# One product of the first mixture of experts as a single float32 matmul in place of three split ones

## The chip, the cores and the metric

The kernel runs on 1 core of one Trainium2 chip. The metric is device time in microseconds (us). A profile is one execution, recorded instruction by instruction. TensorE, the matrix engine, is called PE in it (PEld is its weight load); DVE is the vector engine, ACT the scalar engine, POOL the GpSimd engine, and SP the engine that only issues transfers here.

## The reference

Two decoder layers work on x of 8 x 128 tokens with 128 features. Each layer is attention, cross attention and a feed-forward part, each behind a layer norm. The change is in the feed-forward part of the first layer, a mixture of 16 experts with 8 chosen for each token and one shared expert:

```python
gates = jnp.einsum('bsd,ed->bse', x, gate_w)
scores = jax.nn.sigmoid(gates.astype(jnp.float32))
_, inds = jax.lax.top_k(scores + expert_bias, K)
selected = jnp.take_along_axis(scores, inds, axis=-1)
selected = selected / selected.sum(axis=-1, keepdims=True) * ROUTE_SCALE
combine = jnp.einsum('bske,bsk->bse', jax.nn.one_hot(inds, E), selected)
hg = jnp.einsum('bsd,eid->bsei', x, w_gate)
hu = jnp.einsum('bsd,eid->bsei', x, w_up)
h = jax.nn.silu(hg) * hu
ye = jnp.einsum('bsei,edi->bsed', h, w_down)
y = jnp.einsum('bsed,bse->bsd', ye, combine)
y = y + einsum(silu(x @ shared_gate_w.T) * (x @ shared_up_w.T), shared_down_w)
```

All sizes are 128 (features and hidden units), so each weight matrix is 128 x 128.

## The kernel before

The parts of the network run one after the other. Inside one, each engine runs its own instruction list, and semaphores order them. The first mixture is `mixture0`. All 16 experts are computed for all 1024 tokens, with the hidden layer multiplied by the routing weight, which is zero for the tokens that did not choose the expert. The shared expert is the 17th, number 16.

The tokens are cut into two halves of 512 columns. A **unit** u is one expert and one half: u = 2 x expert + half, so there are 34 units, 0 to 33. For each unit PE makes these products:

* `first_products`: the gate and the up product. Each operand is split in two parts, high and low, of the type F32R, and a product is three matmuls, high x high, high x low and low x high (`product`, lines 870 to 872).
* `weights`: one bf16 matmul that spreads the routing weights of the expert over all partitions (L884). The shared expert has none.
* `last_product`: the down product of `h`, three matmuls again, which add into one PSUM bank per half over all 17 experts.

PE's order is written out by hand: first products of u, weights of u, last product of u - 2. The last product thus runs two units behind, that is one expert behind. The lists of ACT and DVE follow the same order. For a unit ACT makes `g` = silu(gate) (L934), DVE `t` = up x g (L1007) and `h` = t x routing weight (L1012). Then ACT makes `h_hi` (L940, a copy to F32R) and DVE `h_lo` = h - h_hi (L1049). The buffers `g`, `t`, `h`, `h_hi`, `h_lo` exist twice, one for each half.

The weights of an expert (gate, up, down, 192 KB) are loaded by one transfer of SP into `w[j]`, j = expert modulo 2 (L862; the shared expert's is L865). POOL splits them into `w_hi[j]` and `w_lo[j]`: gate and up together (128 x 256) for the first products, which are told by `w_split`, and down (128 x 128), told by `down_split`. Both have a high step (L976) and a low step (L978). SP loads expert e when POOL has split the down matrix of expert e - 2:

```python
sp.wait_ge(S["down_split"], 2 * (2 * i + j - 1))
```

The loop runs over pairs of experts; experts 0 and 1 and the shared one stand outside it. `wait_ge` counts: `y_done` rises by one with each last product, so `y_done >= 2 * (e - 1)` means that all last products of the experts up to e - 2 are finished. `gu_done` counts the first products, `weighted` the finished `h`.

The second mixture of experts (`mixture1`, lines 1410 on) has its own code and isn't touched. Its arrays have the same names in part (`e_h`, `e_y`, `m_w`), and one of its products is a plain float32 one (L1539).

Of the kernel before, what the change touches and what calls it, by code (L numbers as in the profile page):

```python
# [14 lines left out]
F32 = mybir.dt.float32  # L15
BF16 = mybir.dt.bfloat16
F32R = mybir.dt.float32r
# [792 lines left out]
def mixture0(nc, a, tools, layer_norm, x_all, xn_all, xnT_all, consts, tables):  # L810
# [4 lines left out]
    with ExitStack() as top:  # L815
# [2 lines left out]
        one = sb("one", [P, 1])  # L818

        x_hi, x_lo = (sb(n, [P, T], F32R) for n in ("x_hi", "x_lo"))  # L820
        w_hi, w_lo = ([sb(f"{n}{j}", [P, 3, P], F32R) for j in range(2)] for n in ("w_hi", "w_lo"))
        scores, sel, left, mask, comb = (sb(n, [P, B, E0]) for n in ("scores", "sel", "left", "mask", "comb"))
        best = sb("best", [P, B, 8])
        total = sb("total", [P, B])
# [11 lines left out]
        with ExitStack() as st:  # L836
# [1 line left out]
            g = [sb(f"g{j}", [P, HALF]) for j in range(2)]  # L838
            t = [sb(f"t{j}", [P, HALF]) for j in range(2)]
            h = [sb(f"h{j}", [P, HALF]) for j in range(2)]  # L840
            h_hi, h_lo = ([sb(f"{n}{j}", [P, HALF], F32R) for j in range(2)] for n in ("h_hi", "h_lo"))
            yT = sb("yT", [P, 2, HALF])
            gb = [ps(f"gate{j}") for j in range(2)]
            ub = [ps(f"up{j}") for j in range(2)]
# [2 lines left out]

            logits = yb[0][:, 0:B * E0].rearrange("p (b e) -> p b e", b=B)
            turned = yb[1][0:CKV, :].bitcast(BF16)
            names = ("scored", "step", "w_split", "down_split", "one_set", "hi_done", "lo_done",  # L850
                     "gu_done", "c_done", "gated", "times_up", "weighted", "y_done", "yT_out", "turn_done")
            S = {n: sem(n) for n in names} | routing
            block = st.enter_context(nc.Block())
# [3 lines left out]
            @block.sync  # L857
            def _(sp):
                with sp.Fori(1, E0 // 2, 1) as i:
                    for j in range(2):  # L860
                        sp.wait_ge(S["down_split"], 2 * (2 * i + j - 1))
                        sp.dma_start(w[j][:, :, :], a["experts0"][bass.ds(2 * i + j, 1), :, :, :].rearrange(  # L862
                            "o p k m -> (o p) k m")).then_inc(landed[j], 16)
                sp.wait_ge(S["down_split"], 2 * (E0 - 1))
                sp.dma_start(w[0][:, :, :], a["experts0"][E0]).then_inc(landed[0], 16)  # L865

            @block.tensor
            def _(pe):
# [16 lines left out]
                              start=True, stop=True).then_inc(S["c_done"], 1)  # L885

                def last_product(u, half, j, expert, first=False, last=False):
                    if half == 0:
                        pe.wait_ge(S["down_split"], 2 * (expert + 1))
                    pe.wait_ge(S["lo_done"], u + 1)  # L890
                    product(yb[half][:, :], j, 2, h_hi[half][:, :], h_lo[half][:, :], first,
                            last).then_inc(S["y_done"], 1)

                for b in range(B):
                    mm = pe.matmul(logits[:, b, :], xnT_all[:, P * b:P * b + P], gate_w[:, :], start=True, stop=True)
# [32 lines left out]
            @block.scalar  # L928
            def _(act):
                def gate(u, half, free_buffer=True):  # L930
                    act.wait_ge(S["gu_done"], u + 1)
                    if free_buffer:
                        act.wait_ge(S["times_up"], u - 1)
                    act.activation(g[half][:, :], gb[half][:, :], ACT.Silu).then_inc(S["gated"], 1)  # L934

                def high_part(u, half, free_buffer=True):
                    act.wait_ge(S["weighted"], u + 1)
                    if free_buffer:
                        act.wait_ge(S["y_done"], u - 1)
                    act.activation(h_hi[half][:, :], h[half][:, :], ACT.Copy).then_inc(S["hi_done"], 1)  # L940

                for k in range(2):
                    part = slice(HALF * k, HALF * k + HALF)
                    act.activation(x_hi[:, part], xnT_all[:, part], ACT.Copy).then_inc(S["x_hi_done"], 1)
                act.wait_ge(S["logits_done"], 1)
                act.activation(scores[:, :, :], logits, ACT.Sigmoid).then_inc(S["scored"], 1)
                act.preload_act_table(ACT.Silu)
                for k in range(2):
                    gate(k, k, free_buffer=False)
                act.wait_ge(S["wT_turned"], 1)  # L950
                act.activation(wT[:, :], turned, ACT.Copy).then_inc(S["wT_ready"], 1)

                high_part(0, 0, free_buffer=False)
                for k in range(2, 4):
                    gate(k, k % 2)
                    high_part(k - 1, (k - 1) % 2, free_buffer=k == 3)
                with act.Fori(1, E0 // 2, 1) as i:
                    for k in range(4):
                        gate(4 * i + k, k % 2)
                        high_part(4 * i + k - 1, (k - 1) % 2)  # L960
                for k in range(2):
                    gate(LAST + k, k)
                    high_part(LAST + k - 1, (k - 1) % 2)
                high_part(LAST + 1, 1)
                for half in range(2):
                    act.wait_ge(S["y_done"], LAST + half + 1)
                    act.activation(yT[:, half, :], yb[half][:, :], ACT.Copy).then_inc(S["yT_out"], 1)

            @block.gpsimd
            def _(pool):  # L970
                pool.memset(one[:, :], 1.0).then_inc(S["one_set"], 1)
                pool.wait_ge(S["one_set"], 1)

                def split(parts_of, done, e):
                    hi, lo, full = parts_of
                    pool.tensor_tensor(hi, full, free(one[:, :], [[0, full.shape[-1]]]), ALU.mult).then_inc(done, 1)  # L976
                    pool.wait_ge(done, 2 * e + 1)
                    pool.tensor_tensor(lo, full, hi.bitcast(F32), ALU.subtract).then_inc(done, 1)  # L978

                def split_expert(e, j, lot, first=False):  # L980
                    gate_up = [k[j][:, 0:2, :].rearrange("p k m -> p (k m)") for k in (w_hi, w_lo, w)]
                    down = [k[j][:, 2, :] for k in (w_hi, w_lo, w)]
                    pool.wait_ge(landed[j], 16 * (lot + 1))
                    if not first:
                        pool.wait_ge(S["gu_done"], UNITS * (e - 1))
                    split(gate_up, S["w_split"], e)
                    if not first:
                        pool.wait_ge(S["y_done"], UNITS * (e - 1))
                    split(down, S["down_split"], e)

                for j in range(2):
                    split_expert(j, j, 0, first=True)
                with pool.Fori(1, E0 // 2, 1) as i:
                    for j in range(2):
                        split_expert(2 * i + j, j, i)
                split_expert(E0, 0, E0 // 2)

            @block.vector
            def _(dve):
                def hidden(u, half, free_buffer=True, shared=False):  # L1000
                    dve.wait_ge(S["gated"], u + 1)
                    if shared:
                        dve.wait_ge(S["lo_done"], u - 1)
                        dve.tensor_tensor(h[half][:, :], ub[half][:, :], g[half][:, :],
                                          ALU.mult).then_inc(S["weighted"], 1)
                        return
                    dve.tensor_tensor(t[half][:, :], ub[half][:, :], g[half][:, :], ALU.mult).then_inc(S["times_up"], 1)  # L1007
                    dve.wait_ge(S["times_up"], u + 1)
                    dve.wait_ge(S["c_done"], u + 1)
                    if free_buffer:  # L1010
                        dve.wait_ge(S["lo_done"], u - 1)
                    dve.tensor_tensor(h[half][:, :], cb[half][:, :], t[half][:, :], ALU.mult).then_inc(S["weighted"], 1)  # L1012

                for k in range(2):
# [27 lines left out]
                dve.wait_ge(S["step"], 2 * B + 7)  # L1042
                split_weights(dve, comb[:, :, :], E0, parts, rest, S["split"])

                def low_part(u, half, free_buffer=True):
                    dve.wait_ge(S["hi_done"], u + 1)
                    if free_buffer:
                        dve.wait_ge(S["y_done"], u - 1)
                    dve.tensor_tensor(h_lo[half][:, :], h[half][:, :], h_hi[half][:, :].bitcast(F32),  # L1049
                                      ALU.subtract).then_inc(S["lo_done"], 1)  # L1050


                for k in range(4):
                    hidden(k, k % 2, free_buffer=k >= 2)
                    if k >= 1:
                        low_part(k - 1, (k - 1) % 2, free_buffer=k == 3)
                with dve.Fori(1, E0 // 2, 1) as i:
                    for k in range(4):
                        hidden(4 * i + k, k % 2)
                        low_part(4 * i + k - 1, (k - 1) % 2)  # L1060
                for k in range(2):
                    hidden(LAST + k, k, shared=True)
                    low_part(LAST + k - 1, (k - 1) % 2)
                low_part(LAST + 1, 1)
                for half in range(2):
                    dve.wait_ge(S["turn_done"], half + 1)
                    xp = x_all[:, 4 * half:4 * half + 4, :]
# [719 lines left out]
```

## Time and profile before

| | |
|---|---|
| median of 3 runs | 671.01 us (668.39 to 671.37) |
| profiled execution, first to last instruction | 671.6 us |
| its time outside this span | not listed |
| PE busy | 578.1 us (86%) |
| DVE, ACT, POOL busy | 418.3, 324.6, 188.9 us |
| mean granted clock of PE | 0.898 |
| the loop of `mixture0` | about 291 to 377 us of the span |

A row of the timeline has the start, the length, the engine, the line, the operation, out<-in, the shapes and, in brackets, how long the engine had been idle and what ended the wait. Matmuls are pipelined: their recorded length is longer than the distance from one start to the next, so distances of starts are the better measure of PE's pace. PEclk is the clock granted to PE as a share of its full speed.

### The profile page before, as it was taken

How to read it: one execution, taken by the hardware profiler on the slowest of the kernel's cores; microseconds unless marked ns; L12 is line 12 of the kernel's file. 1: busy time of each engine (PE TensorE's matmuls, PEld its weight loads, DVE VectorE, ACT ScalarE, POOL GpSimd, SP SyncE). 2: the span in 40 equal slices, each digit the busy share in tenths (PEclk: the TensorE clock that was granted, in tenths of full speed). 3: DMA queues.
4: the chain of work that ended last, by engine and by line, in shares of the span. 5: the costliest groups of instructions: out<-in, count | busy, mean ns of one | idle time of the engine just before them, and what ended most of it. 6: DMA issues, size and time to landing. Idle time of an engine off the chain costs nothing. (4 is left out here: it accounts for less than half of the span.)

```text
span 671.6 us, 10902 instructions
## 1 busy us (share of the span) xinstructions
PE 578.1 (86%) x3249; PEld 469.4 (70%) x3249; DVE 418.3 (62%) x965; ACT 324.6 (48%) x596; POOL 188.9 (28%) x233
## 2 busy tenths in 40 slices
PE   6698999989779996798888599956699979799996
PEld 3487888889749996566666376835389967577775
DVE  4475665757355554667777616774565536778885
ACT  3354554636145551434433344621355526598883
POOL 1896000000044431424444154011100007254520
PEclk9799999999679996689999868979599976799998
DMA  7500000000000000001110100000000001121201
GB/s 223 125 2 1 0 0 0 0 1 1 0 1 2 0 0 24 23 23 36 36 35 23 47 1 0 1 0 0 1 1 0 0 31 33 33 63 32 63 1 32
DMA packets 18557, 15.08 MB, mean 22 GB/s; under 512 B 2792, under 2 KB 16928, under 8 KB 18304
## 3 DMA queue, kind: packets, MB, share of 16 engines
q1 hardware_dynamic: 17680, 14.12, 7.3%
q10 hardware_dynamic: 848, 0.59, 0.3%
q8 instruction: 15, 0.25, 0.1%
q14 instruction: 14, 0.11, 0.1%
HBM read 14.17 MB, written 0.54 MB: 22 GB/s over the span
## 5 line engine op out<-in xcount | busy, mean ns | idle before, releaser
L172 POOL TENSOR_TENSOR rstd<-var,eps_pow 128x4 f32<-128x4 f32 x12 | 12.3, 1026 | 194.5 <-DVE var L162 194.5
L659 PEld LDWEIGHTS x_pv<-vx,x_pT 77*128 77x128 f32 x512 | 65.2, 201 | 0.0
L659 PE MATMUL x_pv<-vx,x_pT 77*128 (+1 forms) x512 | 64.3, 254 | 0.0
L695 ACT ACTIVATE x_pT<-x_turn 77x512 f32<-77x512 f32 x64 | 37.9, 592 | 50.4 <-PE x_pv L659 50.4
L1735 DVE TENSOR_TENSOR e_h_lo<-kblk,e_h_hi 128x512 fp32r<-128x512 f32 x60 | 49.9, 861 | 16.1 <-ACT e_h_hi L1596 16.1
L1592 ACT ACTIVATE kblk<-e_h,m_b 128x512 f32<-128x512 f32 x64 | 43.6, 688 | 10.3 <-PE e_h L1494 10.2
L641 PE MATMUL x_score<-kblk,x_qs 128*128 (+1 forms) x128 | 48.0, 464 | 0.2 <-ACT x_q L678 0.2
L934 ACT ACTIVATE e_g<-e_gate 128x512 f32<-128x512 f32 x34 | 20.3, 598 | 57.0 <-PE e_up L872 57.0
L572 POOL TENSOR_TENSOR kblk<-ctx_kT,consts 128x1232 f32 x16 | 39.1, 2485 | 9.2 <-POOLq L217 9.2
L650 PEld LDWEIGHTS x_turn<-consts,x_p 128*77 128x77 f32 x256 | 32.1, 148 | 12.5 <-ACT x_p L688 3.1
L650 PE MATMUL x_turn<-consts,x_p 128*77 128x128 f32 x256 | 39.1, 276 | 0.8 <-ACT x_pT L695 0.5
L1596 ACT ACTIVATE e_h_hi<-kblk 128x512 fp32r<-128x512 f32 x64 | 38.7, 635 | 0.0
L177 PE MATMUL n_turned<-consts,xn_all 128*128 128x128 f32 x40 | 12.4, 465 | 30.4 <-DVE xn_all L165 30.4
L400 PE MATMUL a_score<-a_kT,a_qz 128*128 128x128 f32 x256 | 35.4, 282 | 0.7 <-ACT a_v L476 0.7
L400 PEld LDWEIGHTS a_score<-a_kT,a_qz 128*128 128x128 f32 x256 | 33.3, 196 | 2.3 <-ACT a_v L476 1.4
L1007 DVE TENSOR_TENSOR e_t<-e_up,e_g 128x512 f32<-128x512 f32 x32 | 22.0, 688 | 19.4 <-ACT e_g L934 19.4
L182 ACT ACTIVATE xnT_all<-n_turned 128x512 f32<-128x512 f32 x10 | 6.0, 597 | 57.2 <-PE n_turned L177 57.2
L428 PE MATMUL a_pv<-a_v,a_pT 128*128 128x65 f32 x256 | 33.6, 277 | 0.0
L428 PEld LDWEIGHTS a_pv<-a_v,a_pT 128*128 128x128 f32 x256 | 33.2, 201 | 0.3
L976 POOL TENSOR_TENSOR m_w_hi<-m_w,m_one 128x256 fp32r<-128x256 f32 (+1 forms) x34 | 17.8, 523 | 53.5 <-PE e_y L872 50.5
L530 DVE SCALAR_TENSOR_TENSOR a_s<-a_score,w_bias 128x512 f32<-128x512 f32 x32 | 22.0, 689 | 16.4 <-PE a_score L400 16.1
L177 PEld LDWEIGHTS n_turned<-consts,xn_all 128*128 128x128 f32 x40 | 7.3, 182 | 35.1 <-DVE xn_all L165 32.9
(268 smaller groups left out, 1509.2 us busy)
## 6 DMA issues: line engine op xcount, KB each, us to landing
m_w<-in_L_ffn_W SPq DMA_DIRECT2D x16, 256.0 KB, 2.9
m_w<-in_experts SPq DMA_DIRECT2D x17, 192.0 KB, 2.3
su_reversed<-scratch SPq DMA_DIRECT2D x1, 1024.0 KB, 5.9
w_wkv<-in_L_attn_Wkv SPq DMA_DIRECT2D x1, 1024.0 KB, 8.1
a_pick_f<-in_pick SPq DMA_DIRECT2D x1, 768.0 KB
x_all<-in_x SPq DMA_DIRECT2D x1, 512.0 KB, 5.4
w_wq<-in_L_attn_Wq SPq DMA_DIRECT2D x1, 512.0 KB, 6.9
w_wo<-in_L_attn_Wo SPq DMA_DIRECT2D x1, 512.0 KB, 8.9
```

The lines of the kernel that those rows point to most:

```text
L400: mm = pe.matmul(sbk[n % 2][:, h, :], qz[:, hg % 2, h, P * b:P * b + P], kT[:, hg % 2, h // 2, P * b:P * b + P], start=True, stop=True)
L428: mm = pe.matmul(ob[g % 2][:, h, 0:DH0 + 1], pT[g % 2][:, h, :], v[:, hg % 2, b, h, :], start=True, stop=True)
L530: dve.scalar_tensor_tensor(out=s[k][:, :, :], in0=sbk[k][:, :, :], scalar=SC, in1=bias0[:, NG * hg:NG * hg + NG, :], op0=ALU.mult, op1=ALU ...
L572: pool.tensor_tensor(kblk[l][:, bass.ds(b, 1), :].rearrange("p b (h k) -> p (b h) k", h=H), free(ctx_kT[l][:, bass.ds(b, 1), :], [[0, H], ...
L641: pe.matmul(sbk[n % 4], qs[b][:, :], kblk[l][:, bass.ds(2 * i + b, 1), W * hg:W * hg + W], start=True, stop=True).then_inc(S["scores_done" ...
L650: mm = pe.transpose(tb[g % 2][:, h, :], p[g % 4][:, h, :], ident)
L659: mm = pe.matmul(ob[b % 2][:, NG * hg + h, :], pT[g % 2][:, h, :], vx[l][:, bass.ds(2 * i + b, 1), NG * hg + h, :], start=True, stop=True)
L695: act.activation(pT[g % 2][:, :, :], tb[g % 2][:, :, :], ACT.Copy).then_inc(S["turned_out"], 1)
L1007: dve.tensor_tensor(t[half][:, :], ub[half][:, :], g[half][:, :], ALU.mult).then_inc(S["times_up"], 1)
L1592: act.activation(h[half][f], hb[f][:, :], ACT.Gelu, bias=b1[j][:, f:f + 1]).then_inc(S["gelu_done"], 1)
L1596: act.activation(h_hi[half][f - 1][:, :], h[half][f - 1], ACT.Copy).then_inc(S["hi_done"], 1)
L1735: dve.tensor_tensor(h_lo[half][f][:, :], h[half][f], h_hi[half][f][:, :].bitcast(F32), ALU.subtract).then_inc(S["lo_done"], 1)
```

## The change

The down product becomes one plain float32 matmul of `w[j][:, 2, :]` with `h`. `h_hi`, `h_lo` and their steps on ACT and DVE go, and so do the two POOL steps that split the down matrix. The waits that counted `down_split` or `lo_done` now count `y_done` or `weighted`. Since PE reads `w[j]` itself now, the transfer into `w[j]` waits for the last products that read it.

```diff
-        w_hi, w_lo = ([sb(f"{n}{j}", [P, 3, P], F32R) for j in range(2)] for n in ("w_hi", "w_lo"))
+        w_hi, w_lo = ([sb(f"{n}{j}", [P, 2, P], F32R) for j in range(2)] for n in ("w_hi", "w_lo"))
...
                     for j in range(2):
-                        sp.wait_ge(S["down_split"], 2 * (2 * i + j - 1))
+                        sp.wait_ge(S["y_done"], UNITS * (2 * i + j - 1))
                         sp.dma_start(w[j][:, :, :], a["experts0"][bass.ds(2 * i + j, 1), :, :, :].rearrange(
                             "o p k m -> (o p) k m")).then_inc(landed[j], 16)
-                sp.wait_ge(S["down_split"], 2 * (E0 - 1))
+                sp.wait_ge(S["y_done"], UNITS * (E0 - 1))
                 sp.dma_start(w[0][:, :, :], a["experts0"][E0]).then_inc(landed[0], 16)
...
                 def last_product(u, half, j, expert, first=False, last=False):
-                    if half == 0:
-                        pe.wait_ge(S["down_split"], 2 * (expert + 1))
-                    pe.wait_ge(S["lo_done"], u + 1)
-                    product(yb[half][:, :], j, 2, h_hi[half][:, :], h_lo[half][:, :], first,
-                            last).then_inc(S["y_done"], 1)
+                    pe.wait_ge(S["weighted"], u + 1)
+                    pe.matmul(yb[half][:, :], w[j][:, 2, :], h[half][:, :], start=first,
+                              stop=last).then_inc(S["y_done"], 1)
...
-                def high_part(u, half, free_buffer=True):
-                    act.wait_ge(S["weighted"], u + 1)
-                    if free_buffer:
-                        act.wait_ge(S["y_done"], u - 1)
-                    act.activation(h_hi[half][:, :], h[half][:, :], ACT.Copy).then_inc(S["hi_done"], 1)
...
                     split(gate_up, S["w_split"], e)
-                    if not first:
-                        pool.wait_ge(S["y_done"], UNITS * (e - 1))
-                    split(down, S["down_split"], e)
...
                     if free_buffer:
-                        dve.wait_ge(S["lo_done"], u - 1)
+                        dve.wait_ge(S["y_done"], u - 1)
                     dve.tensor_tensor(h[half][:, :], cb[half][:, :], t[half][:, :], ALU.mult).then_inc(S["weighted"], 1)
...
-                def low_part(u, half, free_buffer=True):
-                    dve.wait_ge(S["hi_done"], u + 1)
-                    if free_buffer:
-                        dve.wait_ge(S["y_done"], u - 1)
-                    dve.tensor_tensor(h_lo[half][:, :], h[half][:, :], h_hi[half][:, :].bitcast(F32),
-                                      ALU.subtract).then_inc(S["lo_done"], 1)
```

## Rows read from the trace of the kernel before

**Rows 1.** The page: busy time of each engine, its share of the span, instructions.

```profile
PE 578.1 (86%) x3249; PEld 469.4 (70%) x3249; DVE 418.3 (62%) x965; ACT 324.6 (48%) x596; POOL 188.9 (28%) x233
```

**Rows 2.** Waits between 290 and 370 us: total, times, longest.

```profile
POOL m_w_hi L976 <- PE e_y L872: 50.5, 15, 10.0
...
PE e_y L870 <- DVE e_h_lo L1049: 9.7, 14, 0.7
```

**Rows 3.** The timeline of two units, 301.2 to 304.6 us.

```profile
301.21 0.39 PE L884 MATMUL e_weight<-m_wT,pick 96*128 96x512 bf16 x1
...
302.38 0.40 POOL L976 TENSOR_TENSOR m_w_hi<-m_w,m_one 128x128 fp32r<-128x128 f32 x1 [2.90 <-PE e_y L872]
...
302.76 0.69 DVE L1012 TENSOR_TENSOR e_h<-e_weight,e_t 128x512 f32<-128x512 f32 x1
...
303.29 0.61 POOL L976 TENSOR_TENSOR m_w_hi<-m_w,m_one 128x256 fp32r<-128x256 f32 x1
303.37 1.08 DVE L1049 TENSOR_TENSOR e_h_lo<-e_h,e_h_hi 128x512 fp32r<-128x512 f32 x1
303.50 0.33 SPq L862 DMA_DIRECT2D m_w<-in_experts  x1
...
303.50 0.39 PE L884 MATMUL e_weight<-m_wT,pick 96*128 96x512 bf16 x1
...
304.59 0.47 PE L870 MATMUL e_y<-e_h_hi,m_w_hi 128*128 128x512 f32 x1 [0.70 <-DVE e_h_lo L1049]
```

**Rows 4.** POOL's timeline: the 128 x 256 low steps at 280, 293 and 365 us.

```profile
280.48 0.73 POOL L978 TENSOR_TENSOR m_w_lo<-m_w,m_w_hi 128x256 fp32r<-128x256 f32 x1
...
292.85 1.06 POOL L978 TENSOR_TENSOR m_w_lo<-m_w,m_w_hi 128x256 fp32r<-128x256 f32 x1
...
364.97 1.06 POOL L978 TENSOR_TENSOR m_w_lo<-m_w,m_w_hi 128x256 fp32r<-128x256 f32 x1
```

**Rows 5.** SP's transfers into `m_w`, 262 to 380 us (17 of 192 KB).

```profile
DMA to landing us min/median/max: 2.1/2.3/2.5
```

**Rows 6.** Page, transfers of `mixture1`: KB each, median us from issue to landing.

```profile
m_w<-in_L_ffn_W SPq DMA_DIRECT2D x16, 256.0 KB, 2.9
```

**Rows 7.** `mixture1`, timeline 632.8 to 637.6: a product ends, waiters start, a load lands.

```profile
632.80 0.39 PE L1494 MATMUL e_y<-e_h_hi,m_w_lo 128*128 128x512 f32 x1
...
633.28 1.20 POOL L1634 TENSOR_TENSOR m_w_hi<-m_w,e_one 128x512 fp32r<-128x512 f32 x1 [4.06 <-PE e_y L1494]
633.36 0.33 SPq L1446 DMA_DIRECT2D m_b<-in_b  x1
...
634.39 0.38 SPq L1442 DMA_DIRECT2D m_w<-in_L_ffn_W  x1
...
637.42 1.11 POOL L1634 TENSOR_TENSOR m_w_hi<-m_w,e_one 128x512 fp32r<-128x512 f32 x1 [1.24 <-DMA m_w<-in_L_ffn_W]
```

**Rows 8.** Weight loads of the plain float32 product in `mixture1`, two of eight.

```profile
569.76 0.19 PEld L1539 LDWEIGHTS e_y<-kblk,m_w 128*128 128x128 f32 x1 [0.24 <-ACT kblk L1592]
...
571.91 0.19 PEld L1539 LDWEIGHTS e_y<-kblk,m_w 128*128 128x128 f32 x1 [0.24 <-issue]
```

**Rows 9.** PE's timeline at the end of `mixture0`.

```profile
372.90 0.40 PE L870 MATMUL e_y<-e_h_hi,m_w_hi 128*128 128x512 f32 x1
...
376.44 0.39 PE L872 MATMUL e_y<-e_h_hi,m_w_lo 128*128 128x512 f32 x1
```

**Rows 10.** Windows: length, busy PE, PEld, DVE, ACT, POOL, PEclk, DMA share, GB/s.

```profile
300.00:312.00 12.00, 10.63 (x45) 7.58 (x44) 9.38 (x14) 4.47 (x8) 5.00 (x8) 1.00 0.11 33
...
282.30:289.30 7.00, 6.48 (x15) 4.27 (x16) 4.56 (x7) 1.75 (x3) 0.00 (x0) 0.51 0.00 0
378.20:382.10 3.90, 0.00 (x0) 0.00 (x0) 3.50 (x21) 0.00 (x0) 1.20 (x2) 0.92 0.32 88
382.10:391.40 9.30, 8.31 (x15) 3.98 (x16) 3.34 (x10) 7.04 (x11) 0.85 (x1) 0.50 0.15 48
446.20:449.50 3.30, 3.30 (x4) 1.50 (x5) 2.54 (x7) 0.69 (x1) 0.62 (x1) 0.50 0.00 0
```

More of the change, by code:

```diff
@@ L840, in mixture0 @@
             h = [sb(f"h{j}", [P, HALF]) for j in range(2)]
-            h_hi, h_lo = ([sb(f"{n}{j}", [P, HALF], F32R) for j in range(2)] for n in ("h_hi", "h_lo"))
             yT = sb("yT", [P, 2, HALF])
@@ L849, in mixture0 @@
             turned = yb[1][0:CKV, :].bitcast(BF16)
-            names = ("scored", "step", "w_split", "down_split", "one_set", "hi_done", "lo_done",
+            names = ("scored", "step", "w_split", "one_set",
                      "gu_done", "c_done", "gated", "times_up", "weighted", "y_done", "yT_out", "turn_done")
@@ L951, in _ @@
                 act.activation(wT[:, :], turned, ACT.Copy).then_inc(S["wT_ready"], 1)
-                high_part(0, 0, free_buffer=False)
                 for k in range(2, 4):
                     gate(k, k % 2)
-                    high_part(k - 1, (k - 1) % 2, free_buffer=k == 3)
                 with act.Fori(1, E0 // 2, 1) as i:
@@ L959, in _ @@
                         gate(4 * i + k, k % 2)
-                        high_part(4 * i + k - 1, (k - 1) % 2)
                 for k in range(2):
                     gate(LAST + k, k)
-                    high_part(LAST + k - 1, (k - 1) % 2)
-                high_part(LAST + 1, 1)
                 for half in range(2):
@@ L981, in split_expert @@
                     gate_up = [k[j][:, 0:2, :].rearrange("p k m -> p (k m)") for k in (w_hi, w_lo, w)]
-                    down = [k[j][:, 2, :] for k in (w_hi, w_lo, w)]
                     pool.wait_ge(landed[j], 16 * (lot + 1))
@@ L1010, in hidden @@
                     if free_buffer:
-                        dve.wait_ge(S["lo_done"], u - 1)
+                        dve.wait_ge(S["y_done"], u - 1)
                     dve.tensor_tensor(h[half][:, :], cb[half][:, :], t[half][:, :], ALU.mult).then_inc(S["weighted"], 1)
@@ L1043, in _ @@
                 split_weights(dve, comb[:, :, :], E0, parts, rest, S["split"])
-                def low_part(u, half, free_buffer=True):
-                    dve.wait_ge(S["hi_done"], u + 1)
-                    if free_buffer:
-                        dve.wait_ge(S["y_done"], u - 1)
-                    dve.tensor_tensor(h_lo[half][:, :], h[half][:, :], h_hi[half][:, :].bitcast(F32),
-                                      ALU.subtract).then_inc(S["lo_done"], 1)
                 for k in range(4):
                     hidden(k, k % 2, free_buffer=k >= 2)
-                    if k >= 1:
-                        low_part(k - 1, (k - 1) % 2, free_buffer=k == 3)
                 with dve.Fori(1, E0 // 2, 1) as i:
@@ L1059, in _ @@
                         hidden(4 * i + k, k % 2)
-                        low_part(4 * i + k - 1, (k - 1) % 2)
                 for k in range(2):
                     hidden(LAST + k, k, shared=True)
-                    low_part(LAST + k - 1, (k - 1) % 2)
-                low_part(LAST + 1, 1)
                 for half in range(2):
```

## The prediction

> **What bounds the kernel now.** I read the page first: PE is busy for 86% of 671.6 us [rows 1], so work added to PE, or time in which it stands, tends to show in the end. Then the waits inside the loop of the first mixture. The long entries are POOL waiting for PE, which costs nothing, and fourteen waits of PE for `e_h_lo`, 9.7 us in all [rows 2]. Nothing else stops PE there, so this stage is PE's passes plus these waits. The timeline gives both sizes. One unit is ten passes. From the `weights` matmul at 301.21 to the next at 303.50, with no wait between, are 2.29 us, so 0.229 us a pass [rows 3]. A pair of units, one expert, is longer than 2 x 2.29 = 4.58: POOL's low step of each expert comes at 292.85 for the first of fourteen and at 364.97 for the last, 72.12 / 13 = 5.55 us apart [rows 4]. So 0.97 us of each expert is PE waiting for the low part of `h`. The granted clock is 1.00 in spite of these waits [rows 10].
>
> **What goes and what PE pays.** Three groups of edits, first those without a new wait.
>
> *The waits for `h_lo`.* With `h_hi` and `h_lo` gone, the last product of u needs `h` only. `h` ends at 302.76 + 0.69 = 303.45, 2.24 us after the `weights` matmul of its unit began [rows 3]. The last product that needs it stands behind the `weights` matmul two units on, some 5 us later, so it never waits. That takes away 14 x 0.97 = 13.6 us. At the end of the stage, from 372.90 (three products left, the last waits for the split of the last `h`) to the end of the last pass, 376.44 + 0.23 = 376.67, are 3.77 us [rows 9], of which 9 x 0.23 = 2.07 are passes, so 1.7 more can go. One wait more stands shortly before it, at the last product of unit 31; I put it at 0.7, the longest of the fourteen [rows 2]. Sum: -16.0 us.
>
> *The product itself.* In place of three passes comes a float32 product of 512 columns. The second mixture has four of these in a row, recorded as eight matmuls of two passes' length. Their weight loads stand at 569.76 and, five steps on, 571.91 [rows 8], that is 0.43 us apart. One product is 2 x 0.43 = 0.86 us, against 3 x 0.229 = 0.69. PE pays 0.17 us a unit, 34 x 0.17 = +5.8 us. A unit is now 7 x 0.229 + 0.86 = 2.46, an expert 4.92 us.
>
> *ACT, DVE and POOL.* The 34 steps of `h_hi`, those of `h_lo`, and the 34 on the down matrix go. DVE has 9.38 and POOL 5.00 busy us in a window of 12 [rows 10], and none of them sets PE's pace once `h_lo` is no longer waited for. Worth nothing beyond the -16.0. The new wait of DVE's `h` step for `y_done` is met: the last product of u - 2 follows the `weights` matmul of u at 0.23 us and takes 0.86, so it ends 1.1 us after that matmul's start, and the `h` step begins 302.76 - 301.21 = 1.55 us after it [rows 3]. Were it late, it would cost the difference only.
>
> **What is added: the reload of `w[j]` moves onto PE's path.** This is the step that decides. Before, the transfer for expert e starts when POOL has split the down matrix of e - 2; in the trace SP issues at 303.50, just after POOL's step at 302.38 to 302.78 and its low step, which is a whole expert before PE needs it [rows 3]. Now it waits for `y_done >= 2(e - 1)`, the last product of unit 2e - 3. PE's order is: first products of u, `weights` of u, last product of u - 2. So the last product of 2e - 3 is made at u = 2e - 1, and the next thing in PE's list is the first product of unit 2e. That is the product which needs expert e loaded and split. There is nothing between the event that frees the buffer and the product that needs the new contents, and PE works in order, so everything it has is queued behind. The whole chain of reload and split becomes idle time of PE, for each expert from 2 to 16, fifteen times:
>
> * PE's pass ends, SP issues: 0.33 us. In `mixture1` a last product begins its last pass at 632.80, which ends 0.23 later; POOL, which waits for it, starts at 633.28 and SP at 633.36 [rows 7].
> * Issue to landing 2.3 us, between 2.1 and 2.5 [rows 5].
> * Landing to POOL's start 0.15. There a load is issued at 634.39 and POOL starts 3.03 later [rows 7]; with 2.9 us to landing for that size [rows 6] this leaves 0.13.
> * POOL's high step of 128 x 256, 0.61 [rows 3], and 0.09 to its next step, 0.70 in all. The same step of twice the size took 1.20 and 1.11 us [rows 7], so a tenth more is its upper end.
> * The low step: 1.06 in the loop, where it runs beside `h_lo`, 0.73 where it ran without [rows 4]. In the gap DVE has nothing left to do. I take 0.80.
> * Low step to PE's start: 0.14, as from the end of `h_lo`, 303.37 + 1.08 = 304.45, to PE's 304.59 [rows 3].
>
> Sum 4.42 us, x 15 = +66.3 us. From below, with the fastest landing and low step and POOL's start (0.25) for SP's: 0.25 + 2.1 + 0.13 + 0.67 + 0.73 + 0.10 = 3.98, or +59.7. From above, with the slowest landing, the low step beside DVE, and the hand-overs rounded up: 0.40 + 2.5 + 0.20 + 0.80 + 1.06 + 0.20 = 5.16, or +77.4.
>
> **The clock after each gap.** PE will stand for 4.4 us after each 4.9 us of work. The trace has such a gap: PE stood for 3.9 us, from 378.2 to 382.1, and for the next 9.3 us the granted clock was 0.50, the lower of the two levels, 1.2 GHz against 2.4 [rows 10]. Another start after shorter gaps, at 282.3, worked at 0.51 for 7.0 us, 6.5 of them busy, and one at 446.2 for 3.3 us [rows 10]. Work at 0.50 takes twice as long, so a restart costs half of its low stretch: 1.65 us at 3.3, 3.2 at 6.5. With 4.9 us of work (9.8 if all at the low clock) between gaps, the dense passes should bring the clock back within each expert, as they did in all these rows. I take 2.3 us for each of fifteen, a low stretch of 4.6: +34.5 us. From below 1.35 (shorter than the shortest row by a little, since a fall can come early in the gap) or +20; from above 2.9 or +43.
>
> The Trainium skill speaks against this change in the same place: "TensorE: Matmul & The Clock Gate", section "HAM oscillation — how this bites in real kernels", says that a loop in which the matmuls stop for a load at every tile loses the clock at every tile, and that the extra time is the throttled time times one half. The trace agrees as far as it goes: the gap of 3.9 us was followed by 0.50. By that rule fifteen restarts would each be at the low level, which is what the sum above has; without it the sum would be 34.5 lower.
>
> **The sum.** -16.0 + 5.8 + 66.3 + 34.5 = +90.6 us. The profiled execution is 671.6 us in its span (nothing is listed around it), 0.6 above the median of the runs, so 671.0 + 90.6 = 761.6; I say 761. With all lower values -16.0 + 5.8 + 59.7 + 20 = +69.5 (740.5), with all upper ones -16.0 + 5.8 + 77.4 + 43 = +110.2 (781.2).
>
> **Rivals.**
>
> *The clock holds.* The gaps are there, but no low stretch follows. For it: waits of 0.7 to 1 us do nothing to it [rows 10]. Against: the gap of 3.9 us did. Time: 671.0 + 56.1 = 727. Chance 0.07.
>
> *The clock never comes back.* Each expert's 4.92 us is worked at half speed: 15 x 4.92 = +73.8 in place of 34.5, 801 us. For it: after 282.3 it took 7.0 us [rows 10], and this stage breaks its work off every 10. Against: three restarts in these rows, all ended. Chance 0.06.
>
> *The reload stays hidden, and the kernel is faster.* The place is the wait of SP's list for `y_done`. If the last product of expert e - 2 were finished 4.4 us before the first product of e is due, the chain would lie beside PE's work, as it does now, and only -16.0 + 5.8 = -10.2 us would be left, 661 us. It decides at that point: 4.4 us ahead, and each us less costs 15 us. For it: POOL and SP have much idle time, and the trace has the same transfer hidden. Against: the order of PE's list, which puts the two next to each other. I find no reading of the counts by which it is earlier; 0.03 for a count misread.
>
> *The forecast:* a gap of 4.0 to 5.2 us for each of fifteen experts, with a low stretch behind each, 740 to 782 us. Chance 0.84.
>
> Half a per cent, 3.4 us, is about what a measurement of this kernel can tell from no change; the runs shown differ by 3.0. Slower by more than that: 0.84 + 0.07 + 0.06 = 0.97. Faster: nearly all of the third rival, 0.02, and 0.01 for within it. The range is that of the forecast, 738 to 784, with 2 us more on either side for the rounding of its terms; the rivals outside it hold 0.16.
>
> **What would show it.** In the profile of the changed kernel:
>
> * the longest entry among PE's waits in `mixture0` is for POOL's `m_w_lo`, about 15 times and 4.2 to 4.6 us each; POOL in turn waits for the transfer of `m_w`, and SP for PE's `e_y`;
> * `e_y` has 68 float32 matmul records, 0.43 us apart at full clock, and no wait for DVE;
> * the steps of POOL are 10.5 to 12.5 us apart per expert (9.3 if the clock holds, 14.3 if it never returns), POOL's low step near 0.75;
> * PEclk swings between 0.5 and 1.0 from 292 to some 465 us, where it was 1.00 in the window shown;
> * the stages after it keep their lengths.
>
> Wrong would be the order argument, if PE's waits there are under 1 us; the price of the chain, if the waits are outside 4.0 to 5.2; and the clock term, if PEclk stays above 0.95 in the stage.

## The result, and the profile after

The changed kernel takes 754.45 us (median of 4 runs, 748.14 to 757.37), the kernel before beside it 669.7 (667.11 to 671.37). The ratio is 1.126, with a 95% interval of 1.120 to 1.132. The prediction said 761, between 738 and 784, slower. The profiled execution has a span of 755.5 us, 83.9 longer than before.

The page of the changed kernel:

```profile
span 755.5 us, 10644 instructions
...
PE 610.7 (81%) x3215; PEld 476.7 (63%) x3215; DVE 391.3 (52%) x931; ACT 306.5 (41%) x562; POOL 170.0 (22%) x199
...
PEclk9899999997999757787888787599859996789999
```

DVE, ACT and POOL do less than in [rows 1], as the edit says, and the kernel is longer. PE's share has fallen from 86 to 81%, though its busy time has risen by 33 us: it stands more, and it works slower. The digits of PEclk show where. The ten slices from 283 to 472 us, in which the loop lies, are all at 7 or 8.

The waits of the changed kernel, 288 to 465 us (waited for: total, times, longest):

```profile
POOL m_w_hi L962 <- DMA m_w<-in_experts: 157.8, 15, 19.2
...
PE e_gate L869 <- POOL m_w_lo L964: 62.3, 15, 4.3
...
DVE e_h L994 <- PE e_y L888: 6.8, 10, 0.9
```

and of SP's list in the same stretch:

```profile
SPq L861 <- PE e_y L888: 158.7, 14, 20.2
```

This answers to [rows 2]. PE's fourteen waits for `e_h_lo` are gone, and in their place are fifteen for POOL's split weights. POOL waits for the transfer, and SP, which issues it, for PE's last product. The three waits are one ring.

The timeline of one gap, all engines:

```profile
310.43 0.39 PE L883 MATMUL e_weight<-m_wT,pick 96*128 96x512 bf16 x1
...
310.66 1.02 PE L888 MATMUL e_y<-e_h,m_w 128*128 128x512 f32 x2
...
311.85 0.33 SPq L861 DMA_DIRECT2D m_w<-in_experts  x1
311.98 0.69 DVE L994 TENSOR_TENSOR e_h<-e_weight,e_t 128x512 f32<-128x512 f32 x1
314.38 0.61 POOL L962 TENSOR_TENSOR m_w_hi<-m_w,m_one 128x256 fp32r<-128x256 f32 x1 [9.62 <-DMA m_w<-in_experts]
315.07 0.72 POOL L964 TENSOR_TENSOR m_w_lo<-m_w,m_w_hi 128x256 fp32r<-128x256 f32 x1
...
315.93 0.79 PE L869 MATMUL e_gate<-m_x_hi,m_w_hi 128*128 128x512 f32 x1 [4.25 <-POOL m_w_lo L964]
...
316.52 0.63 PE L870 MATMUL e_gate<-m_x_lo,m_w_hi 128*128 128x512 f32 x1
316.94 0.63 PE L871 MATMUL e_gate<-m_x_hi,m_w_lo 128*128 128x512 f32 x1
```

The float32 product is two matmuls of 0.43, so PE is free at 310.66 + 0.86 = 311.52. SP issues 0.33 us later, POOL starts 2.53 after the issue, its two steps end at 315.79, and PE begins at 315.93, 0.14 later. The gap is 4.41 us. The bracket of its row has 4.25, 0.16 less, since the view counts from the recorded end of the last matmul, 310.66 + 1.02. With 0.16 added to each, the 62.3 us of the list for fifteen gaps become 15 x 4.31 = 64.7 us. POOL's low step is 0.72, with no step of DVE beside it: DVE's last one ends at 312.67. Behind the gap the second and the third pass start 0.42 us apart, not 0.23: the clock is at its lower level.

Windows of the changed kernel (length, busy PE, PEld, DVE, ACT, POOL, PEclk, DMA share, GB/s), which answer to [rows 10]:

```profile
300.00:312.00 12.00, 7.60 (x20) 4.02 (x18) 3.48 (x6) 1.55 (x3) 1.33 (x2) 0.86 0.06 16
300.00:420.00 120.00, 74.14 (x186) 42.41 (x185) 29.05 (x42) 12.30 (x21) 14.69 (x22) 0.80 0.06 18
```

Over 120 us of the loop the mean granted clock is 0.80, where it was 1.00. POOL's timeline gives the length of an expert:

```profile
293.12 0.72 POOL L964 TENSOR_TENSOR m_w_lo<-m_w,m_w_hi 128x256 fp32r<-128x256 f32 x1
...
451.43 0.72 POOL L964 TENSOR_TENSOR m_w_lo<-m_w,m_w_hi 128x256 fp32r<-128x256 f32 x1
```

From the first of fifteen low steps to the last are 158.31 us, 158.31 / 14 = 11.31 us for an expert, against 5.55 in [rows 4].

### The profile page after: what moved, and what is told of

Same layout as the page of the kernel before. It is cut to its first block and busy times, and to the rows that moved or that the text cites. A ratio compares the mean times of both kernels' runs of the same rounds, so it can differ in the third digit from the quotient of the medians.

```text
span 755.5 us, 10644 instructions
## 1 busy us (share of the span) xinstructions
PE 610.7 (81%) x3215; PEld 476.7 (63%) x3215; DVE 391.3 (52%) x931; ACT 306.5 (41%) x562; POOL 170.0 (22%) x199
## 5 line engine op out<-in xcount | busy, mean ns | idle before, releaser
L989 DVE TENSOR_TENSOR e_t<-e_up,e_g 128x512 f32<-128x512 f32 x32 | 22.1, 691 | 116.3 <-ACT e_g L931 116.3
L869 PE MATMUL e_gate<-m_x_hi,m_w_hi 128*128 128x512 f32 x34 | 29.5, 868 | 63.1 <-POOL m_w_lo L964 62.3
L869 PEld LDWEIGHTS e_gate<-m_x_hi,m_w_hi 128*128 128x128 f32 x34 | 9.3, 273 | 82.6 <-issue 77.7
L1561 ACT ACTIVATE kblk<-e_h,m_b 128x512 f32<-128x512 f32 x64 | 43.6, 688 | 10.3 <-PE e_h L1463 10.3
L962 POOL TENSOR_TENSOR m_w_hi<-m_w,m_one 128x256 fp32r<-128x256 f32 x17 | 10.9, 639 | 157.8 <-DMA m_w<-in_experts 157.8
L888 PE MATMUL e_y<-e_h,m_w 128*128 128x512 f32 x68 | 43.0, 723 | 0.0
L428 PEld LDWEIGHTS a_pv<-a_v,a_pT 128*128 128x128 f32 x256 | 31.6, 192 | 0.3
```

Of the source, the lines that this page charges most:

```text
L428: mm = pe.matmul(ob[g % 2][:, h, 0:DH0 + 1], pT[g % 2][:, h, :], v[:, hg % 2, b, h, :], start=True, stop=True)
L869: pe.matmul(out, w_hi[j][:, which, :], hi, start=first, stop=False)
L888: pe.matmul(yb[half][:, :], w[j][:, 2, :], h[half][:, :], start=first, stop=last).then_inc(S["y_done"], 1)
L1561: act.activation(h[half][f], hb[f][:, :], ACT.Gelu, bias=b1[j][:, f:f + 1]).then_inc(S["gelu_done"], 1)
```

## The experiments

The clock of the stages outside the mixture differs a little between runs of one and the same kernel. The first four experiments were timed beside a kernel before of 669.24 us, the last three in a second set, on another chip, beside one of 670.98 us (658.44 to 673.24). So runs that differ by a few us, and runs of different sets, are compared by their traces as well as their medians.

Two theories stood against each other. A: the loss is the reload of `w`, which now stands on PE's path, and the clock that falls in the gaps. B: the loss is the float32 product itself.

**The down matrix with a buffer of its own.**

```diff
-        w = [sb(f"w{j}", [P, 3, P]) for j in range(2)]
+        w = [sb(f"w{j}", [P, 2, P]) for j in range(2)]
+        wd = [sb(f"wd{j}", [P, P]) for j in range(2)]
...
+                sp.wait_ge(S["w_split"], 2)
+                sp.dma_start(w[0][:, :, :], a["experts0"][2][:, 0:2, :]).then_inc(landed[0], 16)
                 with sp.Fori(1, E0 // 2, 1) as i:
                     for j in range(2):
-                        sp.wait_ge(S["y_done"], UNITS * (2 * i + j - 1))
-                        sp.dma_start(w[j][:, :, :], a["experts0"][bass.ds(2 * i + j, 1), :, :, :].rearrange(
-                            "o p k m -> (o p) k m")).then_inc(landed[j], 16)
+                        sp.wait_ge(S["w_split"], 2 * (2 * i + j))
+                        sp.dma_start(w[1 - j][:, :, :], a["experts0"][bass.ds(2 * i + j + 1, 1), :, 0:2, :].rearrange(
+                            "o p k m -> (o p) k m")).then_inc(landed[1 - j], 16)
+                        sp.wait_ge(S["y_done"], UNITS * (2 * i + j - 1))
+                        sp.dma_start(wd[j][:, :], a["experts0"][bass.ds(2 * i + j, 1), :, 2, :].rearrange(
+                            "o p m -> (o p) m")).then_inc(down_landed[j], 16)
...
+                    if half == 0:
+                        pe.wait_ge(down_landed[j], 16 * (lot + 1))
                     pe.wait_ge(S["weighted"], u + 1)
-                    pe.matmul(yb[half][:, :], w[j][:, 2, :], h[half][:, :], start=first,
+                    pe.matmul(yb[half][:, :], wd[j][:, :], h[half][:, :], start=first,
```

> The changed kernel, but the down matrix has its own two buffers and its own transfer. Gate and up of expert e are loaded as soon as POOL has split expert e - 2, a whole expert ahead; only the down matrix waits for the last product that reads its buffer, and it is needed two units later. Theory A (the loss is the reload of w standing on PE's path): the waits of PE for m_w_lo, 62 us in the changed kernel, go to nearly nothing, the clock stays at 1.00 in the loop, and what is left is -16 for the low parts and +5.8 for the product, 671 - 10 = 661 us (656 to 666). Theory B (the loss is the float32 product itself, its length or what it does to the clock): most of the loss stays, above 700 us.

It took 658.96 us (654.92 to 661.18, 6 runs) against 669.24 of the kernel before beside it; ratio 0.984, interval 0.980 to 0.988. All of the loss is gone with the float32 product still in place, so theory B falls. Two windows of its loop (columns as above) and, from its timeline, two of SP's transfers of the down matrix:

```profile
290.00:302.00 12.00, 12.00 (x45) 7.40 (x44) 6.61 (x10) 2.98 (x5) 2.70 (x4) 1.00 0.17 49
302.00:314.00 12.00, 12.00 (x46) 7.34 (x45) 6.59 (x11) 2.98 (x5) 3.91 (x6) 1.00 0.12 33
```

```profile
303.96 0.33 SPq L870 DMA_DIRECT2D m_wd<-in_experts  x1
...
308.89 0.33 SPq L870 DMA_DIRECT2D m_wd<-in_experts  x1
```

PE is busy for 12.00 us of 12, at a clock of 1.00, and has no wait in the loop. An expert takes 308.89 - 303.96 = 4.93 us; the prediction's price for two units was 4.92. This version is faster than both kernels.

**The split product with the late load.** The kernel before, with SP's wait alone changed:

```diff
-                        sp.wait_ge(S["down_split"], 2 * (2 * i + j - 1))
+                        sp.wait_ge(S["y_done"], UNITS * (2 * i + j - 1))
...
-                sp.wait_ge(S["down_split"], 2 * (E0 - 1))
+                sp.wait_ge(S["y_done"], UNITS * (E0 - 1))
```

> The kernel before with one edit: SP loads w[j] when the last products of expert e - 2 are finished, as in the changed kernel. The products stay split in three passes. Theory A: the same 15 gaps of 4.4 us and low clock behind them, so within some 12 us of the changed kernel: 749 us if the waits for the low part of h fall into the gaps (755 - 34 x 0.17), up to 763 if all of them stay. Theory B: within 5 us of the kernel before, 671.

It took 749.69 us (745.84 to 752.22, 4 runs); ratio 1.121, interval 1.115 to 1.127. The reload alone, with no float32 product in this stage, makes the loss. PE's waits:

```profile
PE e_gate L870 <- POOL m_w_lo L978: 62.8, 15, 4.7
...
PE e_y L870 <- DVE e_h_lo L1049: 1.6, 2, 1.4
```

The gaps are the same fifteen. They also swallow the waits for `e_h_lo`, as the lower of the two numbers of theory A had it: DVE makes the low part while PE stands.

**The last product ahead.** The changed kernel with PE's order turned in the second unit of each expert:

```diff
                     for k in range(4):
+                        if k % 2 == 1:
+                            last_product(4 * i + k - 2, k % 2, ((k - 2) % 4) // 2, 2 * i + (k - 2) // 2)
                         first_products(4 * i + k, k % 2, k // 2, i)
                         weights(pick[:, bass.ds(2 * i + k // 2, 1), :], k % 2)
-                        last_product(4 * i + k - 2, k % 2, ((k - 2) % 4) // 2, 2 * i + (k - 2) // 2)
+                        if k % 2 == 0:
+                            last_product(4 * i + k - 2, k % 2, ((k - 2) % 4) // 2, 2 * i + (k - 2) // 2)
```

> The changed kernel with PE's order turned in the second unit of each expert inside the loop: the last product of u - 2 stands ahead of the first products of u, so the buffer of w comes free 1.6 us of PE work earlier (six passes and the routing one, 7 x 0.23). Theory A: each of 14 gaps shrinks from 4.4 to 2.8 us, 755 - 22 = 733 us, or less where the clock falls less often after shorter gaps (down to 705). Theory B: the same work in another order, 750 to 757.

It took 717.67 us (712.24 to 721.07, 4 runs). PE waits 40.2 us in all for `m_w_lo`, fifteen times, against 62.3: 22.1 less, as 14 x 1.6 says. But the time fell by 36.8 us, 15 more than the gaps. The rest is clock, as the starts of the experts on PE's timeline show:

```profile
295.38 0.49 PE L869 MATMUL e_gate<-m_x_hi,m_w_hi 128*128 128x512 f32 x1 [4.23 <-POOL m_w_lo L967]
...
304.75 0.49 PE L869 MATMUL e_gate<-m_x_hi,m_w_hi 128*128 128x512 f32 x1 [2.52 <-POOL m_w_lo L967]
...
306.24 0.65 PE L883 MATMUL e_weight<-m_wT,pick 96*128 96x512 bf16 x1
306.68 3.35 PE L888 MATMUL e_y<-e_h,m_w 128*128 128x512 f32 x4
...
314.24 0.49 PE L869 MATMUL e_gate<-m_x_hi,m_w_hi 128*128 128x512 f32 x1 [2.59 <-POOL m_w_lo L967]
...
321.95 0.49 PE L869 MATMUL e_gate<-m_x_hi,m_w_hi 128*128 128x512 f32 x1 [2.48 <-POOL m_w_lo L967]
...
417.70 0.50 PE L869 MATMUL e_gate<-m_x_hi,m_w_hi 128*128 128x512 f32 x1 [2.81 <-POOL m_w_lo L967]
```

Behind the gap at 304.75 the first passes keep the pace of the full clock, but 1.5 us later the clock falls (306.24 to 306.68 are 0.44 for one pass), and the next expert starts only 9.49 us on. The expert from 314.24 keeps the full pace throughout and takes 7.71, about 4.93 of work and 2.8 of gap. Of the thirteen such distances behind a shortened gap, seven are 9.4 to 9.5 us and six are 7.7 to 8.0. So a gap of this length is followed by a low stretch in about half of the cases, at some 1.7 us each. The point forecast of 733 was too high for that reason: it gave the shorter gaps the clock term of the longer ones. Its lower end, for a clock that falls less often, was 705.

**The gaps filled.** To price the clock by itself, extra passes keep PE at work in each gap. Their result is thrown away by the next product.

```diff
+                    if free_banks:
+                        pe.wait_ge(S["weighted"], u - 1)
+                    if half == 0 and (not isinstance(u, int) or u >= 4):
+                        for _ in range(16):
+                            pe.matmul(gb[half][:, :], x_hi[:, 0:P], x_hi[:, 0:HALF], start=True, stop=True)
                     if half == 0:
                         pe.wait_ge(S["w_split"], 2 * (2 * lot + j + 1))
-                    if free_banks:
-                        pe.wait_ge(S["weighted"], u - 1)
```

> The changed kernel with 16 extra split-type passes of 512 columns on PE in each gap (from expert 2 on), before the wait for the split weights; their result is overwritten by the first product. They take 16 x 0.229 = 3.7 us of the 4.4 us at full clock and so should cost nothing by themselves. If about 30 us of the loss is the clock that falls in the gaps: granted clock near 1.00 in the loop and 755 - 29 = 726 us (722 to 732). If the clock term is something else (other waits behind the gap): no gain, 750 or more.

It took 723.58 us (720.68 to 727.58, 4 runs), 30.9 less than the changed kernel, by adding work. A window of it and one gap in its timeline:

```profile
300.00:420.00 120.00, 113.93 (x438) 76.97 (x437) 35.07 (x51) 15.22 (x26) 17.41 (x26) 1.00 0.07 21
```

```profile
300.19 4.20 PE L878 MATMUL e_gate<-m_x_hi 128*128 128x512 f32 x16
...
303.45 0.61 POOL L965 TENSOR_TENSOR m_w_hi<-m_w,m_one 128x256 fp32r<-128x256 f32 x1 [7.97 <-DMA m_w<-in_experts]
304.14 0.72 POOL L967 TENSOR_TENSOR m_w_lo<-m_w,m_w_hi 128x256 fp32r<-128x256 f32 x1
304.92 0.50 PE L869 MATMUL e_gate<-m_x_hi,m_w_hi 128*128 128x512 f32 x1 [0.52 <-POOL m_w_lo L967]
...
416.09 0.73 POOL L967 TENSOR_TENSOR m_w_lo<-m_w,m_w_hi 128x256 fp32r<-128x256 f32 x1
```

The chain is as long as ever (POOL still waits for the transfer, and the first product starts where it would have), and only the clock is different: 1.00 over 120 us against 0.80. 30.9 / 15 = 2.1 us a gap is what the clock took. The traces agree: from 304.14 to 416.09 are twelve experts of 9.33 us, 1.98 less than the 11.31 of the changed kernel.

**Both.** The order of the third experiment and 10 extra passes (2.3 us) in each of its gaps.

> The changed kernel with both edits: the last product ahead in the second unit, and 10 extra passes (2.3 us at full clock) in each gap, overwritten by the first product. The clock should stay at 1.00, so only gaps count: the kernel with filled gaps (724 us) less 14 x 1.6 = 22, 702 us (698 to 706). The distance to the unfilled one of this order (718) is then what the clock costs there, some 16 us. If the clock cost nothing in that order, 718.

It took 701.15 us (699.02 to 705.05, 4 runs), 22.4 below the filled kernel. POOL's low steps, first and last of fifteen:

```profile
287.90 0.72 POOL L970 TENSOR_TENSOR m_w_lo<-m_w,m_w_hi 128x256 fp32r<-128x256 f32 x1
...
395.47 0.74 POOL L970 TENSOR_TENSOR m_w_lo<-m_w,m_w_hi 128x256 fp32r<-128x256 f32 x1
```

That closes the square: with the clock held, 1.6 us less of gap is worth 22.4 us, which is 14 x 1.6. The clock took 30.9 us with gaps of 4.3 us and 717.67 - 701.15 = 16.5 us with gaps near 2.8. These medians come from two sets, so here is the same from the traces. An expert takes 107.57 / 14 = 7.68 us in this kernel, 1.65 less than in the filled one, and 8.74 in the third experiment's ((417.70 - 295.38) / 14), so there the clock took 14 x 1.06 = 15 us.

**The product twice.** The first experiment's kernel with every down product issued two times; the output is then not the reference's.

```diff
-                    pe.matmul(yb[half][:, :], wd[j][:, :], h[half][:, :], start=first,
+                    pe.matmul(yb[half][:, :], wd[j][:, :], h[half][:, :], start=first, stop=False)
+                    pe.matmul(yb[half][:, :], wd[j][:, :], h[half][:, :], start=False,
                               stop=last).then_inc(S["y_done"], 1)
```

> The kernel with a buffer of its own for the down matrix (659 us), with every down product issued twice, so that the output is not the reference's. If a float32 product costs PE 0.86 us and PE sets the pace there, 34 x 0.86 = 29 more: 688 us (685 to 692), 7.39 us for an expert against 4.93. If PE had slack in that kernel, less than 20 more.

It took 686.78 us (684.39 to 690.55, 4 runs), 27.8 more than with one (in the other set), 0.82 us a product. From its timeline, PE alone, matmuls of two such products, two units apart:

```profile
300.59 1.02 PE L900 MATMUL e_y<-e_h,m_wd 128*128 128x512 f32 x2
...
307.27 1.02 PE L900 MATMUL e_y<-e_h,m_wd 128*128 128x512 f32 x2
```

A unit is (307.27 - 300.59) / 2 = 3.34 us, 0.88 over the 2.46 of one product. So PE has no slack there, and a float32 product costs it 0.86 within the reading. The expectation's 7.39 us for an expert was added up wrongly: 4.93 + 2 x 0.86 are 6.65, and 2 x 3.34 = 6.68 were measured.

**The low part earlier, in the kernel before.** This asks whether the 16 us of waits for `h_lo` could be had without the change.

```diff
                     for k in range(4):
-                        gate(4 * i + k, k % 2)
                         high_part(4 * i + k - 1, (k - 1) % 2)
+                        gate(4 * i + k, k % 2)
...
                     for k in range(4):
-                        hidden(4 * i + k, k % 2)
                         low_part(4 * i + k - 1, (k - 1) % 2)
+                        hidden(4 * i + k, k % 2)
```

> The kernel before with two orders turned inside its loop: ACT makes the high part of unit u - 1 ahead of the gate of u, DVE the low part of u - 1 ahead of the hidden layer of u. The products stay split in three passes, the loads stay early. If the 0.97 us of each expert was the place of the low part in DVE's list, the waits of PE for it (11.6 us) go and the time falls by 10 to 14 us, to 657 us. If DVE, with some 2.3 us of work for a unit of 2.29, becomes the bound in its place, 3 us or less is left of that: 666 to 670.

It took 673.06 us (671.07 to 676.33, 6 runs), beside 670.98 of the kernel before, whose four fastest runs of eleven are 658 to 665: no gain. The waits have moved. Its waits, 290 to 370 us, one turn of DVE and ACT, and two of POOL's low steps ten experts apart:

```profile
ACT e_h_hi L940 <- DVE e_h L1012: 49.7, 28, 2.3
...
DVE e_h_lo L1049 <- ACT e_h_hi L940: 19.9, 27, 0.9
...
PE e_gate L870 <- DVE e_h L1012: 5.7, 19, 0.4
```

```profile
304.08 0.69 DVE L1012 TENSOR_TENSOR e_h<-e_weight,e_t 128x512 f32<-128x512 f32 x1
304.81 0.63 ACT L940 ACTIVATE e_h_hi<-e_h 128x512 fp32r<-128x512 f32 x1 [1.77 <-DVE e_h L1012]
...
305.47 1.12 DVE L1049 TENSOR_TENSOR e_h_lo<-e_h,e_h_hi 128x512 fp32r<-128x512 f32 x1 [0.70 <-ACT e_h_hi L940]
306.52 0.68 DVE L1007 TENSOR_TENSOR e_t<-e_up,e_g 128x512 f32<-128x512 f32 x1
307.23 0.69 DVE L1012 TENSOR_TENSOR e_h<-e_weight,e_t 128x512 f32<-128x512 f32 x1
```

```profile
306.13 1.06 POOL L978 TENSOR_TENSOR m_w_lo<-m_w,m_w_hi 128x256 fp32r<-128x256 f32 x1
...
364.35 1.06 POOL L978 TENSOR_TENSOR m_w_lo<-m_w,m_w_hi 128x256 fp32r<-128x256 f32 x1
```

PE no longer waits for the low part, except once, but its next gate product waits for `h` nineteen times. Neither half of the forecast was quite it: DVE is not full (58.6 us busy of 80 there). What binds is a ring of DVE and ACT: `h`, `h_hi`, `h_lo` of the same unit, then `t` and `h` of the next. Each step of it begins about when the one before ends, and DVE's `t` waits neither for PE nor for ACT. In the kernel before, DVE makes `t` and `h` of the next unit between `h` and its low part, and ACT's `h_hi` is ready by then; here DVE stands idle for it, 0.7 us and more a unit. An expert takes 58.22 / 10 = 5.82 us, 0.27 more than in the kernel before, so in this stage the edit costs a little. In the runs here the waits went when the low part itself went, as in the first experiment; other orders were not tried.

## Why the prediction was right

The forecast was a sum of four terms, +90.6 us; the profiled spans differ by +83.9, the medians by +84.8.

* **The reload on PE's path** (+66.3, 15 x 4.42). It lies on the path for all fifteen experts: right in place. In the gap shown it is 4.41, over all fifteen 4.31 on average, 64.7 us: right in size, 1.6 too high. Each link was right in the gap shown: 0.33 to SP's issue, 2.53 from issue to POOL's start (2.45 forecast), 0.69 and 0.72 for POOL's steps (0.70 and 0.80), 0.14 to PE.
* **The clock** (+34.5, 15 x 2.3). The filled gaps put it at 30.9 us, 2.1 a gap: right in kind, 3.6 us too high. The profiled execution gives the same: of 11.31 us for an expert, less 4.31 for the gap and 4.92 for the work, 2.08 are left. That is a low stretch of 4.2 us, a little shorter than the 4.6 that I took from the rows of restarts.
* **The waits for `h_lo`** (-16.0) **and the product** (+5.8). Together -10.2; the first experiment has just these two and measured 658.96 - 669.24 = -10.3. That the two agree to 0.1 is luck, as single runs of either kernel lie more than 4 us from their medians; but its expert, 4.93 us against 5.55, is 0.62 shorter, and the forecast has 0.97 - 0.34 = 0.63. The product alone is 0.43 us a matmul in the changed kernel too, and 0.82 to 0.88 by doubling it. One slip changes nothing: the wait of 0.7 near the end of the stage is at the last product of unit 30, not 31.

The second experiment made the loss of the first two terms without the product, and the first took it away with the product kept. With the measured sizes the sum is 64.7 + 30.9 - 10.2 = +85.4. The mixture's own length can be read from PE's timeline. It begins in the kernel before, and begins and ends in the changed one, with:

```profile
274.53 0.77 PE L870 MATMUL e_gate<-m_x_hi,m_w_hi 128*128 128x512 f32 x1
```

```profile
272.86 0.77 PE L869 MATMUL e_gate<-m_x_hi,m_w_hi 128*128 128x512 f32 x1
...
457.26 3.00 PE L888 MATMUL e_y<-e_h,m_w 128*128 128x512 f32 x6
```

The last six matmuls end at 457.26 + 6 x 0.43 = 459.84. So the stage took 186.98 us, against 376.67 - 274.53 = 102.14 [rows 9]: 84.8 more. The stages around it, which the change does not touch, were together 0.9 us shorter in the changed kernel's execution, no more than executions of one kernel differ.

The prediction called the new wait of DVE's `h` step for `y_done` met. It is not always: the list has ten such waits, 0.9 us at most. They lie beside PE's work and cost nothing: among PE's waits in that list none is for `h`.

Of the rivals, the clock that holds (727) is what the filled gaps measured, 723.6, so its price was right and its condition was not met. The clock that never comes back (801) did not occur: each expert has passes 0.43 us apart and passes 0.23 us apart. The hidden reload (661) is the kernel of the first experiment, 659.0: it is what the change gives once the buffer that is read late is not the buffer that is needed early.

The rule of the Trainium skill, "TensorE: Matmul & The Clock Gate", section "HAM oscillation — how this bites in real kernels", that a loop which stops for a load at each tile loses the clock at each tile, agrees with the trace for the gaps of 4.1 to 4.4 us, each of which was followed by a low stretch. For gaps near 2.8 us the runs show half of the price, and six experts of thirteen that lost nothing.

Two signs of the prediction missed by a little: I said that PEclk would swing to 465 us, and the stage ended at 460; and that the waits in the list would be 4.2 to 4.6 us each, and they are 4.15 on average, since the list counts 0.16 less than the sum did.

## What to carry to other kernels

When an edit lets an engine read a buffer directly that was only a source for copies before, the buffer is held longer: find the instruction that frees it in that engine's list, and the instruction that needs the next contents. If nothing stands between them, transfer, preparation and all hand-overs become idle time for each turn of the loop, however many buffers there are by name; give the operand that is read late its own buffer and its own transfer, as the first experiment did. A gap of several us on TensorE has a second price behind it, the slower clock, and passes that do nothing are a quick way to measure it.

## What the runs showed of the hardware

* Adding 240 passes to the gaps made the kernel 30.9 us faster (754.45 to 723.58), the granted clock going from 0.80 to 1.00 in the loop.
* The price of the clock does not go with the number of gaps alone: 30.9 us for fifteen of about 4.3 us, 15 to 16.5 us when fourteen of them were 1.6 us shorter. About half of the shorter gaps had no low stretch behind them, and behind others it began only after several passes at full pace.
* POOL's low step took 1.06 us beside DVE's low part [rows 4] and 0.72 with DVE idle. DVE's low part took 1.08 there, and 0.68 where POOL was not at work. It is this pair that slows down, not any work of DVE: in the first experiment POOL's step ran beside DVE's `t` and took 0.73. Removing the low part made POOL's step shorter too. One row of the kernel before, then two of the first experiment:

```profile
294.71 0.68 DVE L1049 TENSOR_TENSOR e_h_lo<-e_h,e_h_hi 128x512 fp32r<-128x512 f32 x1
```

```profile
303.36 0.69 DVE L1000 TENSOR_TENSOR e_t<-e_up,e_g 128x512 f32<-128x512 f32 x1 [1.05 <-ACT e_g L942]
303.53 0.73 POOL L975 TENSOR_TENSOR m_w_lo<-m_w,m_w_hi 128x256 fp32r<-128x256 f32 x1
```
